# Late weights, earlier weight turns, own banks and a second quotient buffer in a two-layer attention and expert kernel

## What is computed

```
x = x + xattn0(_layernorm(x), ctx, ctx)        # 16 heads of 16
x = x + ffn0(_layernorm(x))                    # router over 40, 32 real experts, top 6
x = x + xattn1(_layernorm(x), ctx, ctx)
x = x + ffn1(_layernorm(x))                    # 4-bit feed-forward, 704 wide

def ffn0(x):
    scores = softmax(x @ classifier.T)
    w = 2.5 * scores of the top 6 of (scores + bias), else 0
    out = x * w[:, 32:].sum(-1)                # eight "zero" experts pass x through
    for e in range(32):
        gate, up = split(x @ Wgu[e].T)
        out += w[:, e] * (silu(gate) * up @ Wd[e].T)

def fp4_quant_dequant(x):                      # blocks of 16 along the last dim
    scale = max(max|x| / 6, 1e-12)
    q = nearest of 0, .5, 1, 1.5, 2, 3, 4, 6 to |x / scale|
    return q * sign(x) * scale

def ffn1(x):
    gate, y = fp4(x) @ fp4(w_gate).T, fp4(x) @ fp4(w_up).T
    return fp4(silu(gate) * y) @ fp4(w_down).T
```

## Time and profile before

| | us |
|---|---|
| median of 3 runs | 998.67 |
| the runs | 998.26 to 1001.34 |
| the profiled execution | 1005.61 |
| its span, first to last instruction | 1003.8 |
| PE, DVE, ACT, POOL busy | 898.1, 626.4, 437.4, 304.1 |
| granted PE clock, mean | 0.951 of 2.4 GHz |

### The profile page before, as it was taken

How to read it: one execution, slowest core, us unless ns; L and a number is a source line. 1 busy time by engine, 2 the same in 40 slices (tenths; PEclk the granted TensorE clock), 3 DMA queues, 4 the chain that set the end, 5 groups by cost and what they waited for, 6 DMA issues and landing times.

```text
span 1003.8 us, 19829 instructions
## 1 busy us (share of the span) xinstructions
PE 898.1 (89%) x7228; PEld 685.1 (68%) x7228; DVE 626.4 (62%) x1317; ACT 437.4 (44%) x946; POOL 304.1 (30%) x311
## 2 busy tenths in 40 slices
PE   2997799999997978999999967799999996699996
PEld 1764687878876747878888844587878874366664
DVE  3455577878854594545545465566777764678872
ACT  0442466666664561111111112466666675345442
POOL 8003466767782260000000004000000001476673
PEclk9998799999998798999999977999999999999998
DMA  9788644444333469121111204345565500000000
GB/s 258 219 238 203 113 93 92 93 93 93 62 106 98 138 214 250 46 67 32 32 32 48 65 3 82 74 85 112 107 117 109 106 27 21 0 11 16 16 10 22
DMA packets 98157, 90.45 MB, mean 90 GB/s; under 512 B 43554, under 2 KB 85410, under 8 KB 97954
## 3 DMA queue, kind: packets, MB, share of 16 engines
q1 hardware_dynamic: 98066, 89.25, 36.6%
HBM read 69.36 MB, written 19.63 MB: 89 GB/s over the span
## 4 chain that ended last, share of the span: by engine, by line
PE 72%; DVE 12%; DMA 5%; POOL 3%; ACT 3%; issue 2%; SPq 2%; DVEq 0%; POOLq 0%; ACTq 0%
PE ps L988 13%; PE ps L805 8%; PE ps L859 8%; PE ps L791 8%; PE ps L994 7%; PE ps L819 7%; PE ps L1062 3%; DMA Qz<-mT 3%; PE ps L709 3%; PE ps L1078 2%; PE ps L868 2%; POOL Pr L645 2%; PE ps L779 2%; PE ps L828 1%; DMA X<-x_in 1%
## 5 line engine op out<-in xcount | busy, mean ns | idle before, releaser
L1444 DVE TENSOR_REDUCE ext<-ps 112x2 f32<-112x750 f32 x256 | 232.6, 933 | 66.5 <-PE ps L791 63.4
L1175 ACT ACTIVATE Pr<-ps 125x448 f32<-125x448 f32 x384 | 199.2, 542 | 88.5 <-PE ps L805 75.0
L805 PE MATMUL ps<-Qz,Kp 98*125 98x224 f16 x768 | 130.7, 265 | 14.0 <-DMA Qz<-mT 11.7
L791 PE MATMUL ps<-Kp,Qz 96*112 96x375 f16 x512 | 122.6, 332 | 5.8 <-DMA Qz<-qscr 4.9
L805 PEld LDWEIGHTS ps<-Qz,Kp 98*125 98x125 f16 x768 | 94.8, 137 | 47.2 <-DMA Qz<-mT 15.9
L859 PE MATMUL ps<-wv,ctx 128*125 128x256 f32 x384 | 120.7, 400 | 1.9 <-DVE xT L1417 1.0
L599 POOL TENSOR_TENSOR X<-X,bo 112x256 f32 x32 | 22.5, 724 | 284.6 <-DVE Pr L1362 233.0
L1585 DVE TENSOR_TENSOR Pr<-Pr,ps 128x336 f32<-128x336 f32 (+2 forms) x86 | 32.7, 381 | 88.9 <-ACT Pr L1257 73.8
L819 PE MATMUL ps<-Pr,Vx 125*32 125x112 f32 x3072 | 86.9, 261 | 0.0
L819 PEld LDWEIGHTS ps<-Pr,Vx 125*32 125x32 f32 x3072 | 71.4, 110 | 14.9 <-ACT Pr L1175 10.3
L1589 DVE SCALAR_TENSOR_TENSOR X<-ps,W,X 112x256 f32<-112x256 f32 x167 | 70.7, 477 | 17.3 <-PE ps L994 17.3
(11 more groups left out here) (176 smaller groups left out, 1417.1 us busy)
## 6 DMA issues: line engine op xcount, KB each, us to landing
ctx<-ctxT SPq DMA_DIRECT2D x56, 375.0 KB, 3.7
Kp<-kscr SPq DMA_DIRECT2D x96, 187.5 KB, 4.8
kscr<-ksp SPq DMA_DIRECT2D x24, 375.0 KB, 4.2
Pr<-wexp SPq DMA_DIRECT2D x20, 384.0 KB, 4.2
Qz<-qscr SPq DMA_DIRECT2D x174, 28.0 KB, 4.1
expert<-wexp SPq DMA_DIRECT2D x12, 384.0 KB, 3.9
Pr<-ctxT SPq DMA_DIRECT2D x8, 375.0 KB, 4.5
kscr<-Pr SPq DMA_DIRECT2D x8, 375.0 KB, 3.9
```

The lines of the kernel that those rows point to most:

```text
L791: last = mm(ps[0:S, 2 * (p % 2) + u, 0:M], Qz[0:96, q0 + u * S:q0 + (u + 1) * S], Kp[0:96, k0:k0 + M], start=True, stop=True)
L805: last = mm(ps[0:KC, 4 + k % 2, u * 2 * S:(u + 1) * 2 * S], Kp[0:98, k0:k0 + KC], Qz[0:98, q0:q0 + 2 * S], start=True, stop=True)
L1175: A(Pr[g % 2][0:KC, j, GI * t:GI * t + GI, :].rearrange("r h q -> r (h q)"), ps[0:KC, 4 + k % 2, 0:GI * S], ACT.Exp, scale=scale).then_inc ...
L1444: V.tensor_reduce(ext[0:S, 2 * p:2 * p + 2], ps[0:S, 2 * (p % 2):2 * (p % 2) + 2, 0:M], AX_X, red).then_inc(row_maximum_taken, 1)
```

## The change

Six parts, made together.

1. **Late weights.** `X` comes in two DMAs, 4 batches and 12, and DVE takes the statistics of the 4 first, of the 12 after the third layer norm. PE starts once `wk`, `bqk` and the first context are there. The 15 DMAs of the feed-forward weights and of layer 1's and the router's weights are issued after `flatten(0)`.
2. **Quantising** starts one pass later; the last pass does two sixteenths.
3. **X scaled by two engines**: DVE takes batches 0 to 7, ahead of the mask; ACT takes 8 to 15, in two pieces among its last key copies.
4. **Own banks** for the rest of an expert, by the expert's parity; two waits go.
5. **Weight turns** move from the feed-forward into layer 1's front, as the steps "weight" of `PE_FRONT` and of the new `ACT_FRONT`. The turned weights lie in other tiles now.
6. **Feed-forward**: two buffers `qrh[par]`, `qch[par]`; another order on POOL and DVE; statistics of 10 tiles, and x of tile 0, ahead of the last `normalise` and `residual` of attention 1, with ACT's `x_magic(0)` ahead of its last `values_turned`.

```diff
-PE_FRONT = "turn project turn project turn R R project R R turn R R project R R M V V V V W W"
+PE_FRONT = "weight weight weight weight weight weight weight turn project weight weight weight weight weight turn project turn R R project R R turn R R project R R M V V V V W W"
+ACT_FRONT = "weight weight weight weight weight weight weight turned high weight weight weight weight weight turned high turned high turned high"
...
 @block.sync
             weight(wk[0], attn[0]["wk"], first_weights_loaded)
+            sp.dma_start(bqk[0][:, :], attn[0]["bqk"]).then_inc(first_weights_loaded, 16)
             load_ctx(0, 0)
-            sp.dma_start(X[:, :], x).then_inc(x_loaded, 16)
+            sp.dma_start(X[:, 0:XA * D], x[:, 0:XA * D]).then_inc(x_loaded, 16)
+            load_ctx(1, 1)
+            weight(wq[0], attn[0]["wq"], query_weights_loaded)
+            sp.dma_start(X[:, XA * D:], x[:, XA * D:]).then_inc(x_rest_loaded, 16)
...
                 flatten(0)
+                if l == 0:
+                    load_late_weights()
...
 @block.gpsimd
-            def h_over(i):
+            def h_over(i, par):
                 pool.wait_ge(h_scales_ready, i + 1)
-                wait_from(pool, hq_ready, i)
-                over(qrh, hf, rch, NH, h_divided)
+                if not isinstance(i, int) or i >= 2:
+                    pool.wait_ge(hq_ready, i - 1)
+                over(qrh[par], hf, rch, NH, h_divided)
...
             def ffn_batch(i, par, left=3):
-                h_over(i)
                 if left >= 2:
                     x_back(i + 2, par)
                 if left >= 3:
                     x_over(i + 3)
+                if left >= 1:
+                    h_over(i + 1, 1 - par)
                 h_back(i, par)
...
 @block.tensor
                         pe.wait_ge(first_gated, e + 1)
-                        if e >= 2:
-                            pe.wait_ge(first_added, e - 1)
-                        if e % 2 == 0 and e > 0:
-                            pe.wait_ge(rest_added, rest_n.now() + 2)
+                        if e >= 1:
+                            pe.wait_ge(first_added, e)
...
-                                    if k == 1:
-                                        pe.wait_ge(first_gated, min(e + 2, ER))
...
 @block.scalar
                     for n in range(4, B):
                         next_keys_high(n)
+                        if n in (B - 3, B - 2):
+                            act.wait_ge(x_factors_ready, 1)
+                            for b in range(B // 2, 3 * B // 4) if n == B - 3 else range(3 * B // 4, B):
+                                xb = X[:, b * D:(b + 1) * D]
+                                A(xb, xb, ACT.Identity, scale=zw[0:S, b:b + 1], bias=zb[0:S, b:b + 1]).then_inc(x_scaled, 1)
...
 @block.vector
                     dve.wait_ge(first_weights_loaded, NWK)
+                    dve.wait_ge(x_rest_loaded, 16)
+                    norms(False, XA, B)
...
+                if l == 1:
+                    tile_norms(0, FIRST)
+                    x_scales(0, 0)
+                    x_exponents(0)
+                    x_round(0)
+                    x_scales(1, 1)
                 normalise(g0 + B - 1)
                 residual(g0 + B - 1, B - 1)
...
             def ffn_batch(i, par, left=3, sums=True):
+                h_exponents(i, par)
                 if left >= 2:
                     x_exponents(i + 2)
-                if sums:
-                    ffn_sum(i - 2)
-                h_exponents(i)
                 if left >= 3:
                     x_scales(i + 3, 1 - par)
+                if sums:
+                    ffn_sum(i - 2)
                 if left >= 2:
                     x_round(i + 2)
-                h_round(i)
                 if left >= 1:
                     gate_h(i + 1, 1 - par)
+                h_round(i, par)
```

More of the change, by code:

```diff
@@ L883, in _ @@
                     values = iter([(j, c) for j in range(NJ) for c in range(C2)])
[L884 removed]
+                    turns, projects, weights = iter(range(NG)), iter(range(NG)), iter(range(len(TURNS)))
                     for step in ((PE_FRONT if l else PE_FIRST) if b < 0 else PE_ORDER).split():
[L886 removed]
+                        if step == "weight":
+                            turn_weights(next(weights))
+                        elif step == "turn":
                             turn_group(next(turns))
@@ new lines, in _ @@
+                    weights, turned, high = iter(range(len(TURNS))), iter(range(NG)), iter(range(NG))
+                    for step in ACT_FRONT.split():
+                        if step == "weight":
+                            weights_out(next(weights))
+                        elif step == "turned":
+                            q = next(turned)
+                            t = 4 if q else 0
+                            act.wait_ge(group_turned, q + 1)
+                            A(xTs[q], ps[:, t:t + 2, 0:QG * S], ACT.Copy).then_inc(group_xT_copied, 1)
+                        elif step == "high":
+                            q = next(high)
+                            act.wait_ge(group_projected, q + 1)
+                            for m in range(C2):
+                                last = A(qsps[:, q, :, m, 0, :], ps[:, (6 if q else 2) + m, 0:QG * S].rearrange(
+                                    "p (b q) -> p b q", q=S), ACT.Identity, bias=bqk[1][:, m:m + 1])
+                            last.then_inc(group_high_ready, 1)
```

388 lines of the change are left out of this document (198 added, 190 removed).

## The result

| | before | after |
|---|---|---|
| median in the same session, 4 runs each | 1000.0 | 1038.43 |
| the runs | 998.26 to 1002.96 | 1030.4 to 1039.64 |
| the profiled execution, its span | 1005.61, 1003.8 | 1030.4, 1028.6 |
| PE, DVE, ACT, POOL busy | 898.1, 626.4, 437.4, 304.1 | 905.5, 642.8, 439.1, 306.2 |
| granted PE clock, mean | 0.951 | 0.955 |

The ratio is 1.036, interval [1.031, 1.041]: slower, and 34 us above the forecast of 1004, outside its range. A second look at the same kernel gave 1.031 [1.028, 1.035].

The account below looks back on a forecast made before the run. PE was taken as nearly always busy, so edits pay only where it waits. Terms -6 + 4.5 + 3 - 1 - 2 - 4.5 - 9 + 17 + 3 = +5, carried to the median of 998.67, gave 1004 us, range 988 to 1018.

Parts of the forecast that it names:

- The loop, +17: Feed-forward loop, ten tiles: a new ring through PE, DVE and POOL takes a tile from 9.5 to 11.2 us; +17.
- First stage, -6: Start of the kernel: PE's third keys begin at 26 instead of 32.22; -6 us, between -9 and +2.
- Late loads, +4.5: Attention 0: the moved loads delay the second flatten's DMA, which lands at 121 to 126; +4.5 us, from +1 to +7.
- Quantising, +3: Router's norms: DVE's steps run beside a busy POOL and some wait for it; +3 us, between 0 and +5.
- X by two engines, -1: Ahead of the experts: ACT takes DVE's place as what comes last, ending at 378.3; -1 us, between -4 and +2.
- Own banks, -2: Expert changes: three changes to even experts after a rest save 0.6 us each, no other wait appears; -2 us.
- Weight turns in the front, -4.5: Layer 1's front: turns fill PE's idle time, so projections meet the upper clock level; -4.5 us, between -8 and 0.
- Entry of the feed-forward, -9: Feed-forward's start: first gate at 841.3 instead of 850.07, x rounded at 835.8; -9 us, between -11 and -6.
- The memsets hold DVE, and the port is exclusive: Rival for first stage and loop: first stage +2 instead of -6, tile 11.9, 1019 us; chance 17%.
- No port waits: Rival for loop and quantising: DVE and POOL run side by side, tile 10.5, quantising 0.5, 994 us; chance 28%.
- PE stays the bound: Rival for the loop: the ring closes with slack and the tile stays at 9.5, 987 us; chance 12%.
- The clock rival: Rival for the loop: PE's idling ahead of h's turn drops its clock, up grows over 1 us, 1019 us; chance 5%.

Follow-up runs that it names:

- back_first: Changed kernel, DVE rounding h(i) ahead of gating h(i+1) and POOL doing `h_back(i)` ahead of `h_over(i+1)`; 1017.3 us, ratio 1.013 to before.
- old_loop: Changed kernel with before's order of the feed-forward loop on POOL and DVE, two buffers kept; 1010.56 us, ratio 1.0066 to before.
- best_undo: best with the weight turns back in the feed-forward and `X` scaled by DVE alone; 995.81 us, ratio 0.992 to before.
- spread: best with late loads issued one to four at a time behind the first stage's last context and later flattens, `X` by DVE alone; 978.93 us, ratio 0.976.
- spread_banks: spread with the changed kernel's own banks and waits for the rest of an expert; 976.45 us, ratio 0.973 to before.
- best: as_before plus the `Kp` memset in pieces behind the fifth layer norm and low halves of batches 0 and 1 ahead of late norms; ratio 0.982 to before.
- as_before: old_loop with loads early, quantising a pass earlier, before's banks, and DVE's entry to the feed-forward rearranged; 990.78 us, ratio 0.9873 to before.
- xexp_early: Changed kernel with DVE's `x_exponents(i+3)` ahead of `h_round(i)`; 1043.83 us in two runs, ratio 1.040 to before.
- both_rings: xexp_early with PE's up(i+1) also ahead of the turn of h(i-1); 1021.16 us in two runs, ratio 1.018 to before.

## Why the prediction was wrong, point by point

- **The loop, +17: right** (17.6, tile 11.33 for 11.2), with the ring through PE as one of two. back_first and old_loop cut it and got 19 and 26 us back. What the working missed is that DVE's two exponent steps would be held in full and close a ring of nearly the same length through ACT, whose silu came 0.3 us behind up. That the size came out so near is partly luck: the 0.7 us added on top of 10.5 stood for DVE's steps holding POOL, and POOL lost only 0.6 (0.43 in `h_over`, 0.15 in the last multiplication); the rest of the 0.8 over 10.5 lay in PE's and ACT's steps, which the sum had shorter. Between the profiled runs the loop's order costs 21 us (1029.87 and 1008.66), between the medians 26, in a session whose slower runs have the lower mean clock.
- **First stage, -6: the step that failed** was "I take -6": it weighed a memset that overlapped a step of 0.17 us for 0.08 us against the rule that either blocks the other, and took the overlap for evidence. Taken the other way the term was +2; it measured +2.1. The Trainium skill (SBUF — State Buffer, Who interferes with whom) has it that either blocks the other for the whole instruction, and the trace agrees: 10.12 us beside a memset of 10.09. The data did come early (8.62), and with the memset moved the keys came at 26.61 for a forecast 26.
- **Late loads, +4.5: mechanism right, size off** (+7.5). The second flatten's scores came at 126.31, of which 2.1 us are the first stage's, so the wait itself was inside its bounds. But PE came out of 5.3 us of idling at a lower clock, and its next `project_out` stood at 138.06 instead of 128.91, another 2.9 us later (granted clock 0.70 over 126 to 136). The sum had no term for that.
- **Quantising, +3: right** (3.3), by the steps named: two of 1.53 and 1.44 us beside POOL, and one more at 326.4, 2.7 us in all. How many steps are held depends on where POOL stands: in two kernels with the same late quantising it was 0.4 and 0.6.
- **X by two engines, -1: wrong sign** (+1.0; 0.7 by best_undo). I had ACT end at 378.3 in before's positions; it ended at 380.1. The step that failed is the start of batch 14's key copies, taken as in before: ACT waited 1.92 us for them (385.39), 1.7 us later than counted, because PE's projections ran at the lower level (7.01 us for sixteen matmuls, 5.21 at 371.29), with 4.2 us of idling ahead of the `used` matmul.
- **Own banks, -2: wrong** (+1.1 in this profile, some +2 over all). About 0.6 was gained at single changes (additions 2.22 apart instead of 2.83). "No other wait appears" holds only for experts with a rest; in a run of experts without one, the new wait is for the addition just issued. Such experts follow each other by 1.31 us in the kernel before and often by 1.54 in this one. The times of spread and spread_banks don't confirm a loss.
- **Weight turns in the front, -4.5: right in this pair** (-4.3), but the comparison on best gives 1.2, and with the turns in it the front takes 37.5 to 42.0 us from kernel to kernel. The size is not confirmed.
- **Entry of the feed-forward, -9: the step that failed** was "x rounded at 835.8". It counted ACT's `x_magic` as the last thing awaited, and left out that DVE's norms can only start behind the statistics that residual of batch 14 feeds (840.64 after, 8.4 us of steps and hand-overs behind them). -3.4 came. From `normalise` to the gate another 1.0 was lost: behind 7.4 us of idling PE's four matmuls of `project_out` took 2.04 us instead of 1.12. as_before shows that the gain was there to be had, over 10 us, by another place in DVE's order.
- **Rivals.** "The memsets hold DVE, and the port is exclusive" (17%) was true in its first half (+2) and for DVE's exponent steps, not in its tile of 11.9: `h_over` was held for 0.43 us only, since the rounding beside it had begun 0.25 us earlier and took 0.83. Its 1019 had the forecast's entry, late loads, banks and `X`, which were off by 14 us together, less the 3 that attention 1 gained. "No port waits" and "PE stays the bound" fell. The clock rival is seen in a neighbour of this kernel.

## What to carry to other kernels

Follow a reordered loop as a ring on every engine that it touches; a buffer more is worth nothing if another wait closes first. A load's cost is what stands behind it on its queue, and what PE's clock does after the wait: place loads a few at a time where nothing urgent follows. A helper step moved ahead of a critical one must be ready by then on its own inputs; here the gap one step earlier was free.

## What was not expected of the hardware

- A POOL memset of 10.09 us held a DVE step of 4 elements for 10.12 us, while DVE's BATCH_NORM_STATS2 ran undisturbed beside the same memset in the kernel before. Beside pieces of 0.9 us a layer norm took 0.64 to 1.14 us instead of 0.41.
- It goes both ways: POOL's `h_over` took 1.82 to 1.90 us beside one rounding by DVE and 2.0 to 2.1 beside an exponents step and a rounding (xexp_early, both_rings), instead of 1.39.
- An idle time of PE of 2.5 us in a loop was followed by the lower clock in some tiles (up 4.22 instead of 2.53), one of 1.35 us in the same place by none in the changed kernel's two profiles.
